# Ten weight loads of a constant ahead of each PSUM wait in the last stage's row maxima

## The reference, cut to what matters

```
logits = jnp.einsum('bqhd,bkhd->bhqk', q * scale, k)

def masked_attn(tok_mask):
    key_mask = jnp.concatenate([jnp.ones((Bx, REG), bool), tok_mask], axis=1)
    l = jnp.where(key_mask[:, None, None, :], logits, -jnp.inf)
    a = jax.nn.softmax(l, axis=-1)
    return jnp.einsum('bhqk,bkhd->bqhd', a, v)
x_pos = masked_attn(pos)
x_neg = masked_attn(~pos)
...
return out @ W_proj + b_proj
```

## Time and profile before

| | |
|---|---|
| runs | 1534.29, 1526.98 and 1534.84 us; median 1534.29 us |
| profiled execution | span 1534.1 us (0.2 us below the median run; no other time of it is given) |
| mean granted TensorE clock | 0.921 of full |
| PE busy, share of span | 1336.9 us, 87% |
| PEld busy | 1103.0 us, 72% |
| DVE busy | 976.1 us, 64% |
| ACT busy | 649.8 us, 42% |

### The profile page before, as it was taken

How to read it: one execution, slowest core, us unless ns; L and a number is a source line. 1 busy time by engine, 2 the same in 40 slices (tenths; PEclk the granted TensorE clock), 3 DMA queues, 4 the chain that set the end, 5 groups by cost and what they waited for, 6 DMA issues and landing times.

```text
span 1534.1 us, 27793 instructions
## 1 busy us (share of the span) xinstructions
PE 1336.9 (87%) x11854; PEld 1103.0 (72%) x11854; DVE 976.1 (64%) x1785; ACT 649.8 (42%) x806; POOL 424.2 (28%) x405
## 2 busy tenths in 40 slices
PE   6899998999999999997799789879978958878885
PEld 6788888888878889995387558747756846646563
DVE  3776758768675447776566836766674546567573
ACT  6554546554533336652344145234423531432413
POOL 5140120301324725665033413703421230000000
PEclk9999999999999999997799799979989965988879
DMA  9361210101052207862002000200200020010000
GB/s 294 138 222 32 48 34 18 47 18 49 4 224 69 93 18 259 275 208 81 1 1 75 28 1 17 79 8 1 75 1 1 12 113 22 22 56 15 1 15 15
DMA packets 46138, 103.33 MB, mean 67 GB/s; under 512 B 4336, under 2 KB 26480, under 8 KB 45120
## 3 DMA queue, kind: packets, MB, share of 16 engines
q1 hardware_dynamic: 42944, 93.18, 18.4%
q0 software_dynamic: 3072, 8.39, 1.7%
HBM read 64.79 MB, written 36.77 MB: 66 GB/s over the span
## 4 chain that ended last, share of the span: by engine, by line
PE 70%; DVE 19%; ACT 5%; issue 2%; POOL 2%; DMA 1%; SPq 0%; another core or an unknown queue 0%; POOLq 0%; DVEq 0%; ACTq 0%
PE ps L816 9%; DVE sm L1832 9%; PE ps L117 7%; PE ps L115 7%; PE ps L116 7%; PE ps L1275 4%; PE ps L1269 4%; PE ps L130 4%; PE ps L1014 4%; PE ps L135 4%; PE ps L131 4%; PE ps L998 3%; ACT m L1695 2%; PE ps L1250 2%; DVE m L1821 2%
## 5 line engine op out<-in xcount | busy, mean ns | idle before, releaser
L1447 ACT ACTIVATE m<-ps 128x1024 f32<-128x1024 f32 (+4 forms) x208 | 166.1, 813 | 288.5 <-PE ps L117 109.5
L1832 DVE TENSOR_REDUCE sm<-ps 128x8 f32<-128x2048 f32 (+1 forms) x128 | 193.5, 1532 | 67.3 <-PE ps L1250 36.6
L1821 DVE TENSOR_TENSOR r<-ps,r 128x512 fp32r<-128x512 f32 (+1 forms) x159 | 116.2, 737 | 135.5 <-ACT r L1447 131.8
L2476 POOL TENSOR_SCALAR sm<-sm 128x2 f32<-128x2 f32 x40 | 8.8, 219 | 697.2 <-DVE sm L1850 697.2
L1447 ACT ACTIVATE r<-ps 128x512 fp32r<-128x512 f32 (+1 forms) x159 | 100.8, 639 | 221.3 <-PE ps L816 120.7
L1695 ACT ACTIVATE m<-ps 128x2048 f32<-128x2048 f32 x64 | 119.6, 1877 | 175.2 <-PE ps L1269 175.2
L816 PE MATMUL ps<-cst,m 128*77 128x128 f32 (+2 forms) x1024 | 137.7, 279 | 17.9 <-DVE m L1821 4.7
L816 PEld LDWEIGHTS ps<-cst,m 128*77 128x77 f32 (+2 forms) x1024 | 115.5, 147 | 42.2 <-issue 15.1
L1250 PE MATMUL ps<-m 32*128 32x256 f32 x1024 | 109.9, 567 | 33.0 <-DVE sm L1832 25.7
L1250 PEld LDWEIGHTS ps<-m 32*128 32x128 f32 x1024 | 67.6, 271 | 67.3 <-DVE sm L1832 49.0
L1269 PE MATMUL ps<-m 32*128 32x256 f32 x1024 | 88.2, 472 | 31.4 <-DVE m L2248 24.0
(11 more groups left out here) (322 smaller groups left out, 3613.8 us busy)
## 6 DMA issues: line engine op xcount, KB each, us to landing
raw<-wu_dram SPq DMA_DIRECT2D x20, 768.0 KB
keep_dram<-m SPq DMA_DIRECT2D x8, 768.0 KB, 3.7
m<-keep_dram SPq DMA_DIRECT2D x8, 768.0 KB, 4.2
xs_dram<-gsq SPq DMA_DIRECT2D x2, 2944.0 KB, 18.1
ys_dram<-m SPq DMA_DIRECT2D x23, 256.0 KB, 2.5
room<-wu_dram SPq DMA_DIRECT2D x7, 768.0 KB, 4.8
rt<-xs_dram SPq DMA_DIRECT2D x16, 256.0 KB, 3.1
w1raw<-w_dram SPq DMA_DIRECT2D x1, 3840.0 KB, 11.8
```

The costliest lines, as they stand in the source:

```text
L1447: return act.activation(o, i, ACT.Copy)
L1821: return dve.tensor_tensor(o, a, b_, op)
L1832: return dve.tensor_reduce(o, i, AX.X, op, **kw)
```

## The change

`maxima_of` gets an argument `idle`. With it, TensorE is given that many weight loads of 127 columns of `ones`, read as bfloat16, ahead of the wait for the previous group's maxima, for c = 1, 2 and 3. No matmul uses these weights: each row-tiled matmul has its own load. `fa` passes 10, `a1` passes nothing, so only the last stage has them: 8 batches x 3 groups x 10 = 240 loads.

```diff
+            def keep_busy(n):
+                for _ in range(n):
+                    pe.ldweights(ones.bitcast(BF16)[:, 0:127])
+
-            def maxima_of(st, b, v, sig, dve_):
+            def maxima_of(st, b, v, sig, dve_, idle=0):
                 for c in range(4):
                     if c:
+                        keep_busy(idle)
                         pe.wait_ge(*dve_.at(b, f"nm{c - 1}"))
...
                 pe.wait_ge(*act_.at(b, "ex"))
-                yield from maxima_of(st, b, v, sig, dve_)
+                yield from maxima_of(st, b, v, sig, dve_, 10)
```

## The result

The first comparison gave 1545.36 us (median of 4 runs, 1541.52 to 1558.08) against 1530.79 us for the kernel before (4 runs): 14.6 us more, ratio 1.0119 with a 95% interval of 1.0075 to 1.0163. The forecast was 1552, up 17.5 us, with a range of 1533 to 1560. Both intervals lie above 1: the change makes the kernel slower by about 1%.

A forecast was written before the change was run, and what follows sets the result against it. TensorE, then VectorE's six reductions bound a round. Four cold rounds cost 16.8 us; high clock could spare 4.3 (12.5), cold attention starts add 4.8 (21.6); 17.5 was taken: 1534.3 + 17.5 = 1552 us, range 1533 to 1560.

The forecast's parts named there:

- Price of a pack: Ten unused loads on TensorE in the last stage take 1.07 us at the low clock, 0.6 at the high.
- Where a pack begins: Behind a cold maxima group, loads start 2.01 us after the group's start and end at 3.08.
- Rival C: In the maxima, loads begin while the group still streams; a step costs 0.28 us, total 1543 us; chance 0.13.
- First pack: Loads ahead of stream 0's second group, where TensorE is the limit, add 1.07 us a round.
- A round that is cold throughout: A last-stage round wholly at the low clock costs 4.2 us more, 16.8 for four.
- The high clock in the maxima: Steps at the high clock cost nothing, sparing up to 4.3 us; the clock should rise later, not earlier.
- The attention's start: Rounds two and four may start the attention at the low clock like one and three: 0 to +4.8 us.
- The stages before: Stages ahead of the last must not change; a difference over 1 us means something else is at work.
- Rival A: Loads count as work and lift TensorE's clock in the last stage: 3.2 us gained, 1531 us; chance 0.14.
- Rival B: Loads overwritten unused are dropped in some nanoseconds, so nearly free: 1534 us, 1530 to 1538; chance 0.08.

The follow-up runs named there:

- e9: Changed kernel with ten loads of 128 columns instead of 127: 1534.34 us, ratio 0.9995 (0.9957 to 1.0032) to the kernel before.
- e3: Changed kernel with loads of 32 rows instead of 128: 1536.88 us, ratio 1.0066 (1.0036 to 1.0096) to the kernel before.
- e0_ten_again: Changed kernel once more, unaltered, beside more runs of the kernel before: 1545.24 us, ratio 1.0078 (1.0041 to 1.0115).
- e5: Changed kernel with twenty loads in a pack instead of ten: 1577.56 us, ratio 1.0296 (1.023 to 1.0363) to the kernel before.
- e4: Kernel before, no loads, first half of product groups c = 1 to 3 computed twice in the last stage: 1526.05 us, ratio 1.0012.

## Why the prediction held, step by step

The time of 1545.36 us lies within the range, and both the direction and the path were as forecast. That the sum came near is in part luck: errors of both signs cancelled. The forecast of 1552 was 6.6 too high. Of this 3.5 us are the base, 1534.3, where four runs of the kernel before have a median of 1530.79; the rest, 17.5 against 14.6, is well inside the interval of the measured change (11.5 to 25 us).

- **Price of a pack**: forecast 1.07 and 0.6 us from fp32 loads, measured 1.14 and 0.64. Right, but by luck in one respect: e9 shows that ten bfloat16 loads of 128 columns take 0.52 us, so the fp32 rows priced the 127-column load only.
- **Where a pack begins**: forecast 2.01 us behind a cold group's start, measured 2.02; a step forecast 3.08, measured 3.17. Rival C (a start at 1.44) is out. The reason given, that the new loads use all 128 rows, was wrong: with 32 rows the start is the same (e3). The 32-row fp32 loads of the small products, however, started at 1.44. Those have their matmuls behind them and the unused ones have not, and the types differ; which of the two counts was not tried, and the cause stays open. The Trainium skill, "TensorE: Matmul & The Clock Gate", Part 3, "The mechanism", says that loads overlap matmuls in flight only where the row groups differ. The start in e3 agrees, since rows 0 to 31 are those of a tile of the group in flight; the start at 1.44 fits it less plainly, since the first of the small products' loads is for rows 0 to 31 too.
- **First pack**: forecast +1.07, measured +1.27 (6.32 against 5.05), and 6.32 to 6.34 in every round of every run with ten loads of 127 columns ahead of the second group. The term was mis-sized by 0.2: 0.07 of it is the longer pack, and the other 0.13 is an overlap that is lost. Before, the group's own loads began 0.14 us before the small products' loads ended (1337.06 + 3.77 = 1340.83), as this line of the trace of before shows:

```profile
1340.69 3.12 PEld L1250 LDWEIGHTS ps<-m 32*128 32x128 f32 x32
```

  With the change the pack begins 0.02 behind those loads and the group's loads 0.01 behind the pack (1339.93). The other runs agree: with five, ten and twenty loads and with ten of 128 columns, the first gap is longer than before by the pack's own length (0.61, 1.14, 2.21 and 0.52 us) and 0.12 to 0.15 more each time.
- **A round that is cold throughout**: forecast +4.2, measured +4.8 in the first round of e0_ten_again. The gaps between its reductions grew by 1.27 for the first pack (forecast 1.07), 0.47 at the third group (0.28), 3 x 0.94 at the next three (3 x 0.85) and 0.27 at the last (0.3). So four cold rounds would have cost 19.3 us and not 16.8.
- **The high clock in the maxima**: forecast "the clock at 0.50 throughout the maxima of most rounds", and that it should rise "later, not earlier". This step failed in the first trace: the clock rose earlier in each round (12.6 us after its start instead of 15.8 in the second), and each round had a high stretch in which two packs cost nothing. In e0_ten_again one round had it for two steps, one for all of them, and two hardly. A round cost +3.1 in the maxima of rounds two and three, and the sum over four rounds was 11.2 and 13.7 us, against 12.5 to 16.8 in my bounds.
- **The attention's start**: forecast between 0 and +4.8. Measured -4.0 in the first trace and 0 in the other. The range of this term had the wrong sign. With it the two traces give 7.2 and 13.7 us for the stage (6.9 and 13.6 by its length), where the two ratios give 14.6 and 12 us over many executions (0.0078 x 1536). So one execution is no measure of this term. Whether the clock is up there goes with how the stage happens to fall against the clock's changes, for both kernels.
- **The stages before**: the prediction said that if they differ by more than 1 us something else is at work. The last stage began 1.4 us earlier in the first trace and 5.7 in the other. This sign was set too tight: unchanged code moved its start by up to 13 us between traces.
- **Rival A**: the direct evidence, dense loads at a low clock, held for loads of 128 rows too (e5). The Trainium skill, same page, Part 1, says that the clock follows how busy the array was. That agrees with e4 if busy means products; unused loads did not count by any sign here.
- **Rival B** (packs nearly free): out, each unused load of 127 columns takes its full 0.11 us.

## What to carry to other kernels

Before filling an idle gap of an engine, ask what stands behind the gap: an instruction ahead of a wait is in the queue also where there is no gap, and here the margin was 0.14 us at the low clock and none ahead of the second group. To raise TensorE's clock, stream products, as e4 did; weight loads that nothing uses took 1.27 us a round where TensorE was the limit and gave nothing back. Even where the clock does rise (0.81 to 0.91 over three rounds, e4), the gain is small when another engine sets the pace, so price it by the wait that ends last and not by the clock's mean.

## What the runs showed of the hardware that was not expected

- Ten bfloat16 loads of 127 columns took 1.14 us at the low clock and 0.64 at the high one; ten of 128 columns took 0.52 and 0.46.
- Unused loads of 32 and of 128 rows both began 2.02 us after the start of a cold tiled group of 2.09, with 0.65 us of idle ahead of them. So did 128-row float32 loads with matmuls behind them (L816 in e3_rows32).
- With the change three rounds of the first trace were alike to 0.01 us (68.29, 68.30, 68.30), with the clock changing at the same places in each. With the clock elsewhere, in the other trace of the same kernel, the rounds took 71.82, 69.00 and 67.20 us. Much of the spread between executions comes with the clock in this way, in the stages before as well as here: e3_rows32, whose last stage began first, had the clock low for 109 us ahead of it, and e9_cols128, where it began last, for 147 us.
